# One DMA transpose for both halves of the attention probabilities, and a new order of VectorE's splits

## The reference, cut to what matters

```python
q_c = rmsnorm(hidden_states @ w_qa, g_qa)
q = (q_c @ w_qb).reshape(b, s, NH, QK).transpose(0, 2, 1, 3)
...
query = jnp.concatenate([q_nope, q_rope], -1)
key_s = jnp.concatenate([k_nope, k_rope], -1)
scores = jnp.einsum('bhqd,bhkd->bhqk', query, key_s) * scaling
attn = jax.nn.softmax(scores, axis=-1)
out = jnp.einsum('bhqk,bhkd->bhqd', attn, v)
out = out.transpose(0, 2, 1, 3).reshape(b, s, NH * VD)
return out @ w_o
```

## Time and profile before

| | |
|---|---|
| median of 3 runs | 2190.82 us (2190.57 to 2195.29) |
| the profiled execution, its own time | 2193.07 us |
| its span, first to last instruction | 2190.9 us |
| TensorE busy | 1991.2 us (91%) |
| VectorE busy | 1342.2 us (61%) |
| ScalarE busy | 794.7 us (36%) |
| transposes by DMA, each 128x512 | 3 x 128 |

### The profile page before, as it was taken

One profiled execution on the slowest core, in us unless ns is written; L12 is line 12 of the kernel. 1 busy time (PEld: TensorE's weight loads), 2 busy tenths in 40 slices (PEclk: granted clock), 3 DMA queues, 4 the chain that ended last, 5 costly groups with the idle time before them and its releaser, 6 DMA issues. The chain is left out here.

```text
span 2190.9 us, 43006 instructions
## 1 busy us (share of the span) xinstructions
PE 1991.2 (91%) x11954; PEld 1083.3 (49%) x11954; DVE 1342.2 (61%) x2838; ACT 794.7 (36%) x2083; POOL 305.6 (14%) x612
## 2 busy tenths in 40 slices
PE   4688888867999999999999999999999999869999
PEld 1344444444555555555555555555555555435554
DVE  3666666644666666666666666666666666555554
ACT  3444444433333333333333333333333333232121
POOL 2455555430000000000000000000000000033321
PEclk8888888888999999999999999999999999979999
DMA  4111111102222222222222222222222111130000
GB/s 133 39 39 38 38 38 38 36 1 87 55 54 71 53 53 53 71 53 53 53 71 53 53 53 71 53 53 53 71 53 53 37 37 36 37 113 37 38 38 39
DMA packets 220865, 115.47 MB, mean 53 GB/s; under 512 B 210576, under 2 KB 210832, under 8 KB 218640
## 3 DMA queue, kind: packets, MB, share of 16 engines
q1 hardware_dynamic: 216496, 86.34, 17.4%
q10 hardware_dynamic: 4320, 28.51, 3.8%
HBM read 56.07 MB, written 8.39 MB: 29 GB/s over the span
## 5 line engine op out<-in xcount | busy, mean ns | idle before, releaser
L1103 PE MATMUL out_ps<-m_h,ot_h 128*128 (+1 forms) x1024 | 390.5, 381 | 15.0 <-issue 8.9
L1104 PE MATMUL out_ps<-m_l,ot_h 128*128 (+1 forms) x1024 | 389.4, 380 | 0.0
L1105 PE MATMUL out_ps<-m_h,ot_l 128*128 (+1 forms) x1024 | 389.1, 380 | 0.0
L956 DVE SCALAR_TENSOR_TENSOR resid<-out_ps,resid 128x512 f32 (+1 forms) x256 | 177.0, 691 | 159.4 <-PE out_ps L1105 155.7
L883 ACT ACTIVATE prob<-s_ps,nmx 128x128 f32<-128x128 f32 x512 | 181.3, 366 | 249.9 <-DVE nmx L976 249.9
L827 ACT ACTIVATE qp_h<-qp_ps 128x512 f16<-128x512 f32 (+1 forms) x126 | 75.2, 597 | 502.6 <-PE qp_ps L1038 502.6
L906 DVE SCALAR_TENSOR_TENSOR qp_l<-qp_ps,qp_h 128x512 f16<-128x512 f32 (+1 forms) x126 | 87.1, 691 | 225.7 <-ACT qp_h L827 225.7
L1281 POOL MEMSET fpower<- 128x1 f32 x1 | 0.1, 99 | 1441.7 <-POOLq L739 1441.7
L1103 PEld LDWEIGHTS out_ps<-m_h,ot_h 128*128 128x128 f16 x1024 | 100.2, 98 | 146.1 <-issue 39.0
L1105 PEld LDWEIGHTS out_ps<-m_h,ot_l 128*128 128x128 f16 x1024 | 100.5, 98 | 114.2 <-issue 1.7
L1104 PEld LDWEIGHTS out_ps<-m_l,ot_h 128*128 128x128 f16 x1024 | 100.2, 98 | 106.6 <-issue 1.1
(11 more groups left out here) (248 smaller groups left out, 4164.4 us busy)
## 6 DMA issues: line engine op xcount, KB each, us to landing
wide<-heads_in ACTq DMA_DIRECT2D x30, 928.0 KB, 4.6
wide<-x_in SPq DMA_DIRECT2D x32, 512.0 KB, 5.7
tower_out<-result SPq DMA_DIRECT2D x16, 512.0 KB, 2.6
stage<-wb_in SPq DMA_DIRECT2D x8, 512.0 KB, 9.6
resid<-wqk_in SPq DMA_DIRECT2D x1, 2304.0 KB, 11.0
zt<-z SPq DMA_TRANSPOSE x128, 2.4
pt_h<-p_h SPq DMA_TRANSPOSE x128, 2.4
pt_l<-p_l SPq DMA_TRANSPOSE x128, 2.4
```

What stands on the lines that cost most here:

```text
L956: dve.scalar_tensor_tensor(out=resid[:, at], in0=out_ps[hf][:, :], scalar=1.0 / (O_S * M_S), in1=resid[:, at], op0=ALU.mult, op1=ALU.add). ...
L1103: pe.matmul(out_ps[hf][:, :], ot_h[:, h, :], m_h[:, at], start=h == 0, stop=False)
L1104: pe.matmul(out_ps[hf][:, :], ot_h[:, h, :], m_l[:, at], start=False, stop=False)
L1105: last = pe.matmul(out_ps[hf][:, :], ot_l[:, h, :], m_h[:, at], start=False, stop=h == HEADS - 1)
```

## The change

The two fp16 halves get one common tile, `halves`, 512 columns each; the turned halves get a common tile `turned`. One DMA transpose of 128x1024 takes the place of two of 128x512. SyncE waits only for `p_lo` before it, and one semaphore, `p_turned`, stands for `hi_turned` and `lo_turned`: ScalarE waits for it before it writes the next `p_h`, VectorE before the next `p_l`, TensorE before the first value matmul. On VectorE the low half of `z` and then `p_l` stand right behind the normalisation, and both halves of the residual addition behind them.

```diff
-        p_h, p_l = sb("p_h", [P, CHUNK], F16), sb("p_l", [P, CHUNK], F16)
-        pt_h, pt_l = sb("pt_h", [P, HEADS, P], F16), sb("pt_l", [P, HEADS, P], F16)
+        halves = sb("halves", [P, 2 * CHUNK], F16)
+        p_h, p_l = halves[:, 0:CHUNK], halves[:, CHUNK:2 * CHUNK]
+        turned = sb("turned", [P, 2 * HEADS, P], F16)
...
             def turn_prob(s):
-                waits = [(p_hi, s + 1)]
+                waits = [(p_lo, s + 1)]
                 if not isinstance(s, int) or s >= 1:
                     waits.append((av_done, s))
                 wait_apart(sp, sp_passed, *waits)
-                sp.dma_start_transpose(pt_h[:, :, :], p_h[:, :]).then_inc(hi_turned, 16)
-                wait_apart(sp, sp_passed, (p_lo, s + 1))
-                sp.dma_start_transpose(pt_l[:, :, :], p_l[:, :]).then_inc(lo_turned, 16)
+                sp.dma_start_transpose(turned[:, :, :], halves[:, :]).then_inc(p_turned, 16)
...
                     if before or j:
-                        act.wait_ge(hi_turned, s * 16)
-                    high(p_h[:, :], prob[:, :, :].rearrange("p h n -> p (h n)"), PR_S, p_hi)
+                        act.wait_ge(p_turned, s * 16)
+                    high(p_h, prob[:, :, :].rearrange("p h n -> p (h n)"), PR_S, p_hi)
...
                     behind = (now, j - 1) if j else (before, QUAD - 1)
+                    if after or j < QUAD - 1:
+                        rope_low(s + 1)
+                    dve.wait_ge(p_hi, s + 1)
+                    if before or j:
+                        dve.wait_ge(p_turned, s * 16)
+                    low(p_l, prob[:, :, :].rearrange("p h n -> p (h n)"), PR_S, p_h, p_lo)
                     if behind[0]:
                         add_out(*behind, 0)
-                    dve.wait_ge(p_hi, s + 1)
-                    if before or j:
-                        dve.wait_ge(lo_turned, s * 16)
-                    low(p_l[:, :], prob[:, :, :].rearrange("p h n -> p (h n)"), PR_S, p_h[:, :], p_lo)
-                    if after or j < QUAD - 1:
-                        rope_low(s + 1)
-                    if behind[0]:
                         add_out(*behind, 1)
...
-                    probs_h, probs_l = (pt[:, :, :].rearrange("p h n -> p (h n)") for pt in (pt_h, pt_l))
-                    pe.wait_ge(hi_turned, s * 16 + 16)
+                    probs_h, probs_l = (turned[:, at, :].rearrange("p h n -> p (h n)")
+                                        for at in (slice(0, HEADS), slice(HEADS, 2 * HEADS)))
+                    pe.wait_ge(p_turned, s * 16 + 16)
                     pe.matmul(av_ps[:, :], kc_h[:, at], probs_h, start=True, stop=False)
                     pe.matmul(av_ps[:, :], kc_l[:, at], probs_h, start=False, stop=False)
-                    pe.wait_ge(lo_turned, s * 16 + 16)
                     pe.matmul(av_ps[:, :], kc_h[:, at], probs_l, start=False, stop=True).then_inc(av_done, 1)
```

More of the change, by code:

```diff
@@ L766, in attention_phase @@
         (prod_done, prod_hi, prod_lo, wr_hi, wr_lo, qp_done, qp_hi, qp_lo, rope_done, rot_step,
-         z_hi, z_lo, zt_turned, sp_passed, s_done, max_step, exp_done, norm_step, p_hi, p_lo, hi_turned, lo_turned,
+         z_hi, z_lo, zt_turned, sp_passed, s_done, max_step, exp_done, norm_step, p_hi, p_lo, p_turned,
          av_done, o_hi, o_lo, out_done, out_added) = (sem(n) for n in (
              "prod_done prod_hi prod_lo wr_hi wr_lo qp_done qp_hi qp_lo rope_done rot_step "
-             "z_hi z_lo zt_turned sp_passed s_done max_step exp_done norm_step p_hi p_lo hi_turned lo_turned "
+             "z_hi z_lo zt_turned sp_passed s_done max_step exp_done norm_step p_hi p_lo p_turned "
              "av_done o_hi o_lo out_done out_added").split())
```

## The result

The changed kernel takes 2172.58 us (median of 4 runs, 2171.45 to 2173.35) against 2192.57 us of the kernel before in runs on the same chip: ratio 0.9908, 95% interval 0.989 to 0.9925. It is 20 us faster, 0.9%.

The account below looks back on a forecast made before the run. The attention phase was taken to run at TensorE's pace, so operand arrival counted; 34.3 us in rounds 1 to 27 plus 6.2 in rounds 28 to 30 made 40.5 us slower, 2231 us, range 2186 to 2252.

Parts of the forecast that it names:

- Issue, I: Issue time of the joined 128x1024 transpose on SyncE's queue: taken as 2.04 us, bounds 1.19 and 2.38.
- rival C: Transpose issue costs 1.19 us at any width, only movement grows: 0 to -4 us, 2187 to 2191 us; chance 12%.
- D: Transpose time fixed altogether, issue 1.19 us, no added movement: 12 to 18 us won, 2173 to 2179 us; chance 10%.
- Movement, M: DMA movement of the joined transpose: double width adds 0.66 us, or nothing at the lower bound.
- the 1.31 us: Time from the end of a transpose's issue to TensorE's start, including the first 0.66 us of movement.
- the prediction's own sum: Earliest start of the value matmuls, counted from the start of `p_h`: 1.53 + 2.04 + 1.31 + 0.66 = 5.54 us.
- step 2: Third of a round's four attention steps: value matmuls at 5.54 against 4.96 us, +0.58 us.
- Step 0: First step of a round: value matmuls at 5.54, `zt` work at 6.85 against 6.16 us, +0.69; 0.84 at row maximum.
- the sum: 1.27 us a round in rounds 1 to 27, 34.3 us, plus 6.2 in rounds 28 to 30: together 40.5 us slower.
- steps 1 and 3: Second and fourth steps of a round: value matmuls at 5.54 against 5.66 and 5.13 us, both counted as 0.
- Part 1: VectorE's new order, `z`, then `p_l`, then both additions: counted as 0.
- Part 2: One transpose for both halves, sent only after `p_l`: its issue starts at 1.53 us instead of 0.72.

Follow-up runs that it names:

- no_zt_wait: Kernel before, with stored latents as operand of the scores' rotary part in place of `zt`, so TensorE doesn't wait for `zt`: 2145.37 us, ratio 0.9786.
- the three-wide one: Changed kernel with `z` of the next step as third part of `halves`, one 128x1536 transpose a step: 2208.46 us, ratio 1.0077 against the kernel before.

## Why the prediction was wrong, point by point

- **Issue, I: the step that failed.** It was put at 2.04 us, between 1.19 and 2.38, from a plain transfer's 0.34 us and the count of packets. It measured 1.23. A plain transfer is another kind of instruction; its issue said nothing on how that of a transpose grows, and twice the pieces made it only 0.04 us longer. The prediction's own sign of being wrong, an issue under 1.5 us, came. Rivals C and D, with I = 1.19, had it nearly right and 22% between them. That the time fell beside D's 2173 to 2179 is luck: D had no added movement (M = 0) and its gain in step 0, and neither came.
- **Movement, M, and the 1.31 us: right.** 0.66 was added and the landing grew from 2.4 to 3.1 (0.04 of it issue). With the measured I the prediction's own sum gives value matmuls at 1.53 + 1.23 + 1.31 + 0.66 = 4.73 (measured 4.85 in step 0) and step 2 untouched at 4.96, as it was.
- **Step 0: the size was off, the chain right.** The values reach the row maximum through `ot_h` and `ot_l`, 4.85 + 2.12 = 6.97; it measured 6.95. So from `p_h` to the row maximum step 0 lost 0.13 us and not the 0.69 of the sum (0.84 at the row maximum); rival C, with the same chain, had next to nothing.
- **"No wait" read as no cost: the second step that failed.** With I right, the sum would still have come to rival C, 0 to -4 us; the kernel gained 20. Where the sum priced `zt`'s lateness, it took the idle time shown at the wait, and in steps 1 and 3 nothing. Between before and after, two rounds got rid of 0.80 us ahead of `zt` and of 1.47 us behind it in the rotary stretches, and took on 0.76 us ahead of the values and 0.23 us, shown as "issue", ahead of a round's first scores: 1.28 us less, where the windows gave 1.27. The 1.47 us, the sequencer's register work that a late `zt` uncovers, have no place in the prediction.
- **"TensorE sat idle for it 26.7 us, 55 times": misread.** It was 16.5 us in 33 waits, counted on two tracks. No term of the sum rests on it.
- **"1.5 us in two rounds is all that any edit can win back": wrong.** no_zt_wait, which leaves out one dependency, takes 2.40 us less, and its whole 85.19 us are less than the 86.06 counted as work. A score matmul on `zt` is shown 0.22 us long while the next starts 0.056 us later, so gaps up to 0.16 us between starts count as busy; for the same matmuls TensorE's busy time fell from 86.06 to 85.15 us. The Trainium skill warns of it (page "Perfetto Trace Analysis", section "Identifying the Most-Contended Engine"): the busy time of pipelined matmuls isn't a good measure of how near the limit an engine is. The fall of the busy time agrees.
- **Part 1 counted as 0: right alone, in the steady rounds** (87.57 us in two rounds), and 4 us in the first and last ones, which the sum left out. Part 2's start at 1.53 took the new order for granted; without it the start is 2.17 in one step of eight (and near 1.8 in every step 1, where TensorE comes late anyway), and the whole kernel is 10 us slower.
- **What was to be seen:** the new wait for `turned` came, 0.48 us in one step 0 of two and not over 1 us; in step 2 none. The waits for `zt` are gone. Two rounds took 86.3 us and not 90.

## What to carry to other kernels

Before an operation is widened, look for what in the trace bounds its fixed part, and where only another kind of instruction gives a row, hold both ends of the price as equally likely: here one number, the issue, chose between 2% slower and no slower. An operand that lands late or just in time costs more than the wait shown where the engine's sequencer has work of its own behind the wait, here 1.8 us of register operations in a loop round: look for that work, compare the stretch behind the wait with the same stretch where the operand was early, and price the lateness by the difference. Reordering one engine and merging two transfers can be worth less each than together, when the merge makes the reordered result the last one needed.

## What the runs showed of the hardware that was not expected

The issue of a DMA transpose from SBUF to SBUF grows little with its width: 1.19, 1.23 and 1.43 us (medians) for 128x512, 128x1024 and 128x1536 in fp16. Movement starts 1.1 to 1.2 us after the issue began at each width, and each 512 columns more land 0.6 to 0.7 us later. The joined transpose of 262 KB landed after 3.1 us. By the fit of the Trainium skill (page "DMA: Bandwidth & Descriptors", section "Anatomy of one DMA — SWDGE (gpsimd) path", for DMAs that GpSimd issues) it would be an estimated 2.6 us; the measurement decides. The two-wide transpose is 0.9% faster than two apart, the three-wide one 0.8% slower than the kernel before, as the values wait for the longer movement. The advice of the Trainium skill (page "DMA: Bandwidth & Descriptors", section "Rules for kernel authors") to coalesce many small transfers into one large one agrees with the first and not with the second.

TensorE's sequencer spends 1.8 to 2.4 us of a loop round's step on the 14 or 15 register operations ahead of the output product, and matmuls that are too short to cover them leave gaps that the profile labels "issue". Taking the wait for `zt` out of TensorE's program (no_zt_wait) saved 47 us, where 27.1 us of idle weight loads, in 42 waits, were shown for it in the whole kernel.
